# First expert phase of an audio tower: its first weights resident in SBUF, copied per tile by ScalarE, and 101 and 103 tiles in place of 104

## The chip, the core and the metric

The kernel runs on one core of one Trainium2 chip. The metric is the device time of one execution in microseconds (us). TensorE (PE), VectorE (DVE), ScalarE (ACT), GpSimd (POOL) and SyncE (SP) each work through a queue of their own and meet only at semaphores. SP issues plain DMAs, POOL the indirect ones, which scatter rows by an index.

## The reference, cut to what matters

The input is 8 sequences of 750 positions with 128 features. A convolution block leaves 748 positions each, so 5,984 tokens. Two layers of attention-like mixing follow, each with a mixture of experts behind it. The first mixture, which the change is about:

```python
scores = xt @ gate_w.T
_, idx = jax.lax.top_k(scores + biases, K)                       # K = 2 of E = 8 experts
h = jax.nn.silu(jnp.einsum('td,edh->eth', xt, w1)) * jnp.einsum('td,edh->eth', xt, w3)   # 128 -> 256
y = jnp.einsum('eth,ehd->etd', h, w2)                            # 256 -> 128
out = jnp.einsum('te,etd->td', comb, y) + shared
```

The second mixture takes the best 2 of 10 experts with one first weight of 128x512, a bias, an elu and a second weight of 512x128. All data is float32.

## The kernel before

Each token goes to two experts, 11,968 pairs in all. The pairs are sorted by expert in DRAM (`rows_in`), each expert's region padded up to whole tiles of 128 rows, and the program runs through a fixed number of tiles, `EXPERT_TILES` = 104, in both expert phases. A row holds 128 features, the place of its result and its gate. How many tiles an expert has is decided while the program runs; the tables `tile_expert`, `tile_col` (the expert times 128) and `tile_row` are written by VectorE, one entry to a tile, and engines read them into registers. Tiles behind the last real one are empty ones.

A tile `u` of the first phase (`experts0`) passes through these steps. The line numbers are those of the profile:

- SP loads its 128 rows (`load_row`, L708, 65 KB) and its expert's first weights w1 and w3, side by side 128x512, 256 KB (`load_w1`, L713).
- PE transposes the rows (`xT`, L990); DVE copies the result to SBUF (`xT`, L1873).
- PE multiplies by w1 and w3 (`up`, L1001: four products, eight matmul records in float32).
- ACT applies silu to one half (`silu`, L1341), DVE multiplies by the other (`u`, L1879).
- PE multiplies by w2 (`down`, L1010, four records); DVE scales by the gate (`y`, L1900).
- POOL keeps place and gate of the row apart (`keep`, L2224 and L2225) and stores the result rows with an indirect DMA (`store`, L2232).

There are 8 slots (`RING`) for rows, first weights and outputs, and 4 sets of PSUM banks (`SLOTS`), so a slot is used again 8 tiles later. Row loads wait for `keep` of the tile 8 before, weight loads for `u` of the tile 8 before, and `keep` and `y` for the store of the tile 8 before. The second weights of all experts (`ew2_0`) already lie in the tensor `wreg`, loaded at the start; the area from column 2048 to 6144 of `wreg` is unused until the phase is over.

The function `turns` sets the order on each engine: in turn `u` an engine does each of its steps for tile `u + AHEAD[step]`. With `xT` 3, `up` and `silu` 2, `u` 1, `down` and `y` 0, PE's turn is `xT(u+3), up(u+2), down(u)`, DVE's is `xT(u+3), u(u+1), y(u)`, POOL's is `keep(u+3), store(u)`. An engine works in this order alone, so a step that waits holds up everything behind it. Eight turns form one pass of a loop; the last pass stands outside it. The class `Steps` counts each engine's finished steps for each slot on a semaphore.

The second expert phase has the same steps, but its first weights and bias come from DRAM (`w_and_b`, 258 KB a tile), ACT copies xT (L1355) and computes four exponentials (L1348), and PE has 18 matmul records where the first phase has 13.

Of the kernel before, what the change touches and what calls it, by code (L numbers as in the profile page):

```python
# [9 lines left out]
I32 = mybir.dt.int32  # L10
ALU = mybir.AluOpType
# [16 lines left out]
assert (PAIRS + (E1 - 1 + 1) * (P - 1)) // P <= EXPERT_TILES  # L28
# [12 lines left out]
EITERS = EXPERT_TILES // SLOTS  # L41
GROUPS = 2
RING = GROUPS * SLOTS
RITERS = EXPERT_TILES // RING
REGION = (B * L + P - 1) // P + 1
# [38 lines left out]
AHEAD = {"xT": 3, "up": 2, "silu": 2, "exp": 2, "u": 1, "down": 0, "y": 0, "keep": 3, "store": 0}  # L84


def turns(eng, stages, begin=None):
# [25 lines left out]
class Steps:  # L113
# [7 lines left out]
    def __init__(self, phases):  # L121
        self.phases, self.base, self.next = phases, {}, {}
        at = {}
        for phase, (iters, count, names) in phases.items():
            assert len(names) <= self.CREDIT
            for lane in self.lanes(count):
                self.base[phase, lane] = at.get(lane, self.CREDIT)
                at[lane] = self.base[phase, lane] + iters * len(names)
# [18 lines left out]
    def end(self, phase):  # L147
# [4 lines left out]
        return [(lane, self.base[phase, lane] + iters * len(names)) for lane in self.lanes(count)]  # L152


def audio_tower(nc, d, out):
    with ExitStack() as ctx:
# [20 lines left out]
        tile_col = sb("tile_col", [P, EXPERT_TILES], I32)  # L177
# [24 lines left out]
        ew2_0 = wreg[:, 0:E0 * HID0]  # L202
        sw13 = wreg[:, 6144:6144 + 512]
# [298 lines left out]
        def chunk_steps(names):  # L502
# [7 lines left out]
            "experts0": (EITERS, SLOTS, ["xT", "up", "down"]),  # L510
            "attention": (ITERS, LANES, ["norm5T", "q0", "q1", "k0", "k1", "v"]
                          + chunk_steps(["sc", "cx"]) + ["out", "norm6T", "rc1", "taps", "scores"]),
            "experts1": (EITERS, SLOTS, ["xT", "up", "down"]),
# [7 lines left out]
            "experts0": (EITERS, SLOTS, ["silu"]),  # L521
            "attention": (ITERS, LANES, ["n5T", "q0", "q1", "k0", "k1"] + chunk_steps(["qb", "kt", "den"])
                          + ["n6T", "rc1", "taps", "kept"]),
            "experts1": (EITERS, SLOTS, ["xT", "exp"]),
# [7 lines left out]
            "experts0": (EITERS, SLOTS, ["xT", "u", "y"]),  # L532
            "attention": (ITERS, LANES, ["h3", "var5", "norm5", "q0", "q1", "k0", "k1", "v"]
                          + chunk_steps(["at", "st"]) + ["h4", "var6", "norm6", "scores"]),
            "experts1": (EITERS, SLOTS, ["u", "y"]),
# [6 lines left out]
            "experts0": (EITERS, SLOTS, ["keep"]),  # L542
            "attention": (ITERS, LANES, ["rstd5", "rstd6"]),
            "experts1": (EITERS, SLOTS, ["keep"]),
# [103 lines left out]
        def _(sp):  # L648
# [50 lines left out]
            def expert_tiles(m, phase):  # L699
# [1657 lines left out]
```

## Time and profile before

| | |
|---|---|
| median of 3 timed runs | 1641.15 us (1637.29 to 1647.4) |
| profiled execution, its own time | 1635.27 us |
| span of the profiled execution | 1633.4 us |
| TensorE busy in the span | 1331.9 us, 82% |
| VectorE, ScalarE, GpSimd busy | 1011.0, 623.3 and 568.2 us |
| first expert phase, first transpose to last store's start | 393.0 to 583.7 us |
| second expert phase, first to last store's start | 1366.8 to 1572.3 us |

All numbers of the rows are of the one profiled execution. A start is in us from the start of the span. PE is the matmul side of TensorE and PEld its weight loads. Behind a row of a timeline stands in brackets how long the engine had been idle and what released it; "remote" is a release that the profile can't pin to an engine's step. The end of a matmul is modelled.

### The profile page before, as it was taken

How to read it: one execution, taken by the hardware profiler on the slowest of the kernel's cores; microseconds unless marked ns; L12 is line 12 of the kernel's file. 1: busy time of each engine (PE TensorE's matmuls, PEld its weight loads, DVE VectorE, ACT ScalarE, POOL GpSimd, SP SyncE). 2: the span in 40 equal slices, each digit the busy share in tenths (PEclk: the TensorE clock that was granted, in tenths of full speed). 3: DMA queues.
4: the chain of work that ended last, by engine and by line, in shares of the span. 5: the costliest groups of instructions: out<-in, count | busy, mean ns of one | idle time of the engine just before them, and what ended most of it. 6: DMA issues, size and time to landing. Idle time of an engine off the chain costs nothing.

```text
span 1633.4 us, 33209 instructions
## 1 busy us (share of the span) xinstructions
PE 1331.9 (82%) x10360; PEld 1114.8 (68%) x10361; DVE 1011.0 (62%) x3372; ACT 623.3 (38%) x1514; POOL 568.2 (35%) x900
## 2 busy tenths in 40 slices
PE   5687595958888828796899869988699798999975
PEld 3475564736888826575687647876487798999963
DVE  6396777663444457765454745647364546988956
ACT  2425445221222204262234513344235225666633
POOL 1114545535777730002200050001400324777742
PEclk9798797988999969998899989989799899999997
DMA  7102200005777630100010010000101134777734
GB/s 232 49 19 70 54 19 24 28 24 156 218 215 220 212 126 1 40 1 20 20 40 2 1 36 24 20 1 8 32 2 36 38 113 115 193 200 192 199 109 152
DMA packets 104747, 133.18 MB, mean 82 GB/s; under 512 B 21127, under 2 KB 61293, under 8 KB 104386
## 3 DMA queue, kind: packets, MB, share of 16 engines
q1 hardware_dynamic: 91330, 107.08, 22.5%
q0 software_dynamic: 13312, 24.74, 4.5%
q8 instruction: 61, 1.00, 0.3%
q14 instruction: 44, 0.36, 0.1%
HBM read 99.28 MB, written 36.51 MB: 83 GB/s over the span
## 4 chain that ended last, share of the span: by engine, by line
PE 56%; DVE 18%; issue 10%; DVEq 4%; ACT 4%; POOL 3%; DMA 2%; another core or an unknown queue 2%; POOLq 1%; SPq 0%; ACTq 0%
PE psum L1152 10%; PE psum L1001 9%; PE psum L1010 7%; PE psum L1091 3%; PE psum L1068 3%; PE psum L990 3%; DVE work L1556 2%; PE psum L1161 2%; PE psum L1113 2%; DVE stats L1539 2%; PE psum L815 2%; PE psum L1210 2%; PE psum L1086 2%; PE psum L1095 1%
## 5 line engine op out<-in xcount | busy, mean ns | idle before, releaser
L1152 PE MATMUL psum<-NT,wreg 128*128 128x182 f32 (+1 forms) x1536 | 265.3, 329 | 15.9 <-issue 7.9
L1152 PEld LDWEIGHTS psum<-NT,wreg 128*128 128x128 f32 x1536 | 251.6, 194 | 24.4 <-issue 13.5
L1001 PE MATMUL psum<-work 128*128 128x128 f32 x1664 | 225.4, 279 | 24.1 <-DVE work L1873 23.0
L2232 POOL DMA_INDIRECT rows_out<-work,expert_row_kept x208 | 206.2, 991 | 107.5 <-issue 37.5
L2181 POOL TENSOR_TENSOR rstd<-var_eps,pack 128x6 f32<-128x6 f32 x40 | 57.7, 1443 | 496.3 <-DVE var_eps L1546 496.0
L1001 PEld LDWEIGHTS psum<-work 128*128 128x128 f32 x1664 | 204.3, 193 | 31.4 <-issue 17.7
L1348 ACT ACTIVATE work<-psum,work 128x128 f32<-128x128 f32 x416 | 118.6, 368 | 64.4 <-PE psum L1001 56.8
L1900 DVE TENSOR_SCALAR work<-psum,expert_row_kept 128x128 f32<-128x128 f32 x208 | 72.7, 349 | 105.3 <-PE psum L990 47.7
L1891 DVE SCALAR_TENSOR_TENSOR work<-psum,work 128x128 f32<-128x128 f32 x416 | 117.1, 344 | 7.8
L815 PE MATMUL psum<-pack,work 128*128 128x128 f32 (+2 forms) x288 | 54.2, 349 | 80.3 <-DVE work L1556 73.7
L1010 PE MATMUL psum<-work 128*128 x832 | 110.2, 275 | 1.4 <-DVE work L1891 1.4
L2200 POOL DMA_INDIRECT rows_in<-N,slot_now x96 | 99.0, 1031 | 28.6 <-issue 28.4
L815 PEld LDWEIGHTS psum<-pack,work 128*128 128x128 f32 (+2 forms) x288 | 45.3, 185 | 90.2 <-DVE work L1556 56.3
L1010 PEld LDWEIGHTS psum<-work 128*128 128x128 f32 x832 | 101.2, 192 | 2.0 <-issue 2.0
L1341 ACT ACTIVATE work<-psum 128x256 f32<-128x256 f32 x104 | 39.3, 383 | 156.3 <-PE psum L1001 108.5
L2195 POOL TENSOR_TENSOR slots_seen<-pack 128x1 f32<-128x1 f32 x16 | 4.1, 255 | 264.2 <-DVE slot_now L1742 250.5
L1949 DVE TENSOR_TENSOR work<-psum,pack 128x1024 f32<-128x1024 f32 (+1 forms) x48 | 56.7, 1192 | 32.5 <-remote 19.1
L1068 PE MATMUL psum<-work 64*128 64x256 f32 (+1 forms) x384 | 57.8, 422 | 17.1 <-DVE work L1984 9.3
L2224 POOL TENSOR_TENSOR keep_seen<-pack 128x1 f32<-128x1 f32 x208 | 51.1, 246 | 53.5 <-PE psum L990 48.6
L1963 DVE TENSOR_TENSOR upd<-psum,pack 128x128 f32<-128x128 f32 x40 | 11.5, 288 | 86.3 <-PE psum L1095 65.8
L1445 ACT COPY pack<-psum 128x384 f32<-128x384 f32 (+1 forms) x64 | 29.9, 470 | 91.4 <-PE psum L1152 81.1
L1010 PE MATMUL psum<-wreg,work 128*128 x416 | 63.4, 275 | 0.9 <-DVE work L1879 0.9
(358 smaller groups left out, 2837.0 us busy)
## 6 DMA issues: line engine op xcount, KB each, us to landing
work<-w_and_b SPq DMA_DIRECT2D x104, 258.0 KB
work<-in_ew SPq DMA_DIRECT2D x104, 256.0 KB
work<-rows_in SPq DMA_DIRECT2D x208, 65.0 KB
work<-rows_out SPq DMA_DIRECT2D x32, 384.0 KB, 4.3
rows_out<-work,expert_row_kept POOLq DMA_INDIRECT x208
work<-in_xT SPq DMA_DIRECT2D x8, 375.0 KB, 4.7
w_and_b<-in_ew SPq DMA_DIRECT2D x1, 2560.0 KB
out<-H SPq DMA_DIRECT2D x8, 320.0 KB
```

The lines of the kernel that those rows point to most:

```text
L815: r = nc.tensor.transpose((acc or v.P)[:, j // 3, c0:c0 + widths[j]], src(j), ident[0:widths[j], 0:widths[j]])
L1001: r_ = mm(v.ps1[:, c * P:(c + 1) * P], v.w1[:, c * P:(c + 1) * P], v.xT, start=True, stop=True)
L1010: r_ = mm(v.psy, v.e[:, c * P:(c + 1) * P], weights[:, bass.ds(which[u] * nh + c * P, P)], start=(c == 0), stop=(m == 0 and c == nh - 1))
L1068: mm(acc[:, :, 0:n], v.QK[2 + g][rows, col], v.QB[rows, g, :, 0:n], start=True, stop=True)
L1152: r = mm(bank[:, half * HALF_PAIRS:half * HALF_PAIRS + p1 - p0], weights[:, m * P:(m + 1) * P], product_input(name, g, k, p0, p1), start=( ...
L1348: r_ = A(v.e[:, c * P:(c + 1) * P], v.ps1[:, c * P:(c + 1) * P], ACT.Exp, bias=v.b1[:, c:c + 1])
L1891: r_ = V.scalar_tensor_tensor(v.e[:, cols], v.ps1[:, cols], v.b1[:, c:c + 1], v.e[:, cols], ALU.add, ALU.max)
L1900: V.tensor_scalar(v.y, v.psy, v.gate, None, ALU.mult).then_inc(dve_done[k], dve.step(phase, "y", k))
L1949: r = V.tensor_tensor(v.AT2[0:n, :, 0:n], v.AB.rearrange("p b (x i) -> p (b x) i", i=P)[0:n, :, 0:n], w("causal")[0:n, 0:n].unsqueeze(1).b ...
L2181: r = G.tensor_tensor(v.rstd[:], v.ve[:], w("minus_half"), ALU.pow)
L2200: G.indirect_dma_start(rows_in[m], bass.IndirectOffsetOnAxis(ap=slot_now[0:n, q, j:j + 1], axis=0), staged(m, q, k)[0:n, j % TILES, :], No ...
L2232: G.indirect_dma_start(rows_out[m], bass.IndirectOffsetOnAxis(ap=v.dest, axis=0), v.y, None, bounds_check=last, oob_is_err=False).then_inc ...
```

## The change

Three things change.

1. All first weights of the first phase (8 experts, 128x4096, 2 MB) are loaded once, at the start of the program, into the free columns of `wreg` (`ew1_0`). SP's 104 loads L713 are gone, and with them SP's read of `tile_expert` and its wait for DVE's `u` in this phase.
2. ACT gets a step `w1`, three tiles ahead: it copies the tile's 512 columns from `ew1_0` to the slot's `w1`, at an offset that it reads from `tile_col` once in 8 tiles. PE's `up` waits for that copy in place of the load.
3. The number of tiles is worked out for each phase (`EXPERT_COUNT`): (11968 + 8*127)/128 = 101 in the first, (11968 + 10*127)/128 = 103 in the second. The last pass has 5 and 7 turns in place of 8, and semaphore counts are adapted. The tables still have 104 entries, and 4 zeros behind `tile_col`.

```diff
-EITERS = EXPERT_TILES // SLOTS
+EXPERT_COUNT = [(PAIRS + ne * (P - 1)) // P for ne in (E0, E1)]
+LAST_ROUND = [n - (RITERS - 1) * RING for n in EXPERT_COUNT]
-AHEAD = {"xT": 3, "up": 2, "silu": 2, "exp": 2, "u": 1, "down": 0, "y": 0, "keep": 3, "store": 0}
+AHEAD = {"w1": 3, "xT": 3, "up": 2, "silu": 2, "exp": 2, "u": 1, "down": 0, "y": 0, "keep": 3, "store": 0}
...
-            if first and t < 0 or last and t >= RING:
+            if first and t < 0 or last and t >= LAST_ROUND[m]:
...
+        ew1_0 = wreg[:, 2048:2048 + E0 * 2 * HID0]
+        experts0_w1_in = sem("experts0_w1_in")
...
             for name, dst in (("sw13", sw13), ("sw2", sw2)):
                 sp.dma_start(dst, d[name]).then_inc(shared_in, 16)
+            sp.dma_start(ew1_0.rearrange("p (x c) -> p x c", x=E0),
+                         d["ew_0"].rearrange("p (x c) -> p x c", x=E0)[:, :, 0:2 * HID0]).then_inc(experts0_w1_in, 16)
             for t in range(3):
                 sp.dma_start(raw_taps[:, t].rearrange("p (g c) -> p g c", g=3),
...
-                    if m == 0:
-                        sp.dma_start(slots[u].w1, d["ew_0"].rearrange("p (x c) -> p x c", x=E0)[
-                            :, bass.ds(x, 1), 0:2 * HID0].rearrange("p a c -> p (a c)")).then_inc(w1_in[u], 16)
-                    else:
-                        sp.dma_start(slots[u].w1b, w1b_1[bass.ds(x, 1)].rearrange("a p c -> p (a c)")).then_inc(w1_in[u], 16)
+                    sp.dma_start(slots[u].w1b, w1b_1[bass.ds(x, 1)].rearrange("a p c -> p (a c)")).then_inc(w1_in[u], 16)
...
                 def up(u, i):
-                    e.wait_ge(w1_in[u], i * 16 + (16 + m * 16 * RITERS))
                     if m == 0:
+                        e.wait_ge(act_done[k], act.at(phase, "w1", k, r))
                         e.wait_ge(dve_done[k], dve.at(phase, "xT", k, r))
...
+                def begin_w1(at, places):
+                    e.reg_load(regs[0:len(places)], tile_col[0:1, bass.ds(at, len(places))])
+                    for u, place in enumerate(places):
+                        which[place] = e.snap(regs[u], min_val=0, max_val=P * (E0 - 1))
+
+                def w1(u, i):
+                    v = slots[u]
+                    k, r = slot_round(u, i)
+                    e.wait_ge(pe_done[k], pe.at(phase, "up", k, r - GROUPS))
+                    nc.scalar.copy(v.w1, ew1_0[:, bass.ds(which[u] * 4, 4 * P)]).then_inc(act_done[k], act.step(phase, "w1", k))
+
+                e.wait_ge(experts0_w1_in, 16)
+                e.wait_ge(dve_route_done, dve_route.at("tables0", "tables", 0, 0))
+                begin_w1(0, range(ahead))
+                turns(e, [("w1", w1), ("silu", silu)], m, lambda i: begin_w1(i * RING + ahead, [(u + ahead) % RING for u in range(RING)]))
```

On SP, in the first expert phase's loop, row loads and weight loads took turns (L708 is a row load, L713 a weight load, `in_ew` the weights in DRAM, ISA a register step that carries a wait):

```order
L736 TENSOR_LOAD tile_expert
L737 REGISTER_ALU
L737 TENSOR_LOAD tile_row
L740 ISA
L707 ISA
L708 DMA work<-rows_in 128x130
L742 ISA
L711 ISA
L713 DMA work<-in_ew 128x512
```

and now, at the same place, only the row loads are left:

```order
L758 TENSOR_LOAD tile_row
L761 ISA
L729 ISA
L730 DMA work<-rows_in 128x130
L729 ISA
L730 DMA work<-rows_in 128x130
L761 REGISTER_ALU
```

So of every two DMAs that SP issued for a tile one is gone, with one of two table reads in a pass.

On ACT, in the same loop, there was one activation for a tile, the silu:

```order
L98 UNCONDITIONAL_BRANCH
L98 ISA
L1341 ACTIVATE work<-psum 128x256 x2
L1339 ISA
L1341 ACTIVATE work<-psum 128x256 x2
```

and now a copy of another 128x512 stands ahead of each, with a table read at the head of a pass:

```order
L1393 TENSOR_LOAD tile_col
L1395 ISA
L1400 ISA
L1401 COPY work<-wreg 128x512
L1366 ISA
L1368 ACTIVATE work<-psum 128x256
L1400 ISA
L1401 COPY work<-wreg 128x512
```

L1401 is the copy of tile `u+3`'s weights and L1368 the silu of tile `u+2`; between them no function table is loaded.

At the start of the program SP gets one DMA, L683, ahead of the three that bring the convolution taps (L686; before, L664 stood right behind L662):

```order
L679 DMA wreg<-in_ew 128x8x256
L682 DMA wreg<-in_sw 128x512
L682 DMA wreg<-in_sw 128x256
L683 DMA wreg<-in_ew 128x8x512
L686 DMA H<-in_conv 128x3x512 x3
```

So everything that SP issues from L686 on stands behind 2 MB more.

## Rows read from the trace of the kernel before

**Rows 1.** The page, its first line.

```profile
span 1633.4 us, 33209 instructions
```

**Rows 2.** Busy time by stretch: start:end, length, engines, granted clock, DMA share, GB/s.

```profile
420.00:570.00 150.00, 129.30 (x1087) 122.73 (x1088) 71.95 (x252) 31.52 (x84) 109.45 (x250) 1.00 0.72 217
1370.00:1570.00 200.00, 197.52 (x1785) 193.59 (x1785) 180.18 (x600) 132.13 (x493) 144.02 (x297) 1.00 0.68 184
```

**Rows 3.** The line L2232, 388 to 590 us: ns min/median/max, starts, idle before.

```profile
L2232 POOL DMA_INDIRECT rows_out<-work,expert_row_kept x104: 971/992/1029, 400.8 to 583.7; - x104
  DVE work L1873: 34.3, 27
```

**Rows 4.** Waits, 393 to 585 us: us in total, times, longest.

```profile
ACT work L1341 <- PE psum L1001: 108.5, 73, 12.6
DVE work L1900 <- remote: 36.8, 17, 2.4
PE psum L1001 <- DVE work L1873: 23.0, 29, 1.1
```

**Rows 5.** Timeline, 469.8 to 474.9 us: start, busy us, engine, line, idle before.

```profile
470.07 1.06 PE L1001 MATMUL psum<-work 128*128 128x128 f32 x8
...
470.56 0.99 POOL L2232 DMA_INDIRECT rows_out<-work,expert_row_kept  x1 [0.16 <-issue]
...
470.96 0.61 PE L1010 MATMUL psum<-wreg,work 128*128 x4
...
471.52 1.06 PE L1001 MATMUL psum<-work 128*128 128x128 f32 x8
471.58 0.20 POOL L2224 TENSOR_TENSOR keep_seen<-pack 128x1 f32<-128x1 f32 x1
...
471.94 0.38 ACT L1341 ACTIVATE work<-psum 128x256 f32<-128x256 f32 x1 [1.84 <-PE psum L1001]
472.06 1.00 POOL L2232 DMA_INDIRECT rows_out<-work,expert_row_kept  x1 [0.16 <-issue]
...
473.43 0.35 DVE L1900 TENSOR_SCALAR work<-psum,expert_row_kept 128x128 f32<-128x128 f32 x1 [2.20 <-remote]
...
474.57 0.99 POOL L2232 DMA_INDIRECT rows_out<-work,expert_row_kept  x1 [1.18 <-DVE work L1873]
```

**Rows 6.** The line L2232 in the second expert phase, 1300 to 1620 us.

```profile
L2232 POOL DMA_INDIRECT rows_out<-work,expert_row_kept x104: 966/991/1030, 1366.8 to 1572.3; - x104
```

**Rows 7.** Waits, 1366 to 1573 us.

```profile
ACT work L1348 <- PE psum L1001: 56.8, 90, 0.8
```

**Rows 8.** DMA, 393 to 585 us: SP's queue (packets, MB, share), its issues of weights.

```profile
q1 hardware_dynamic: 28276, 31.96, 57.5%
...
work<-in_ew SPq DMA_DIRECT2D x96, 256.0 KB
```

**Rows 9.** Groups by line and form on ACT, whole span: busy us, mean ns.

```profile
L1341 ACT ACTIVATE work<-psum 128x256 f32<-128x256 f32 x104 | 39.3, 383 | 156.3 <-PE psum L1001 108.5 <-remote 29.4 <-issue 18.3
L1355 ACT COPY work<-psum 128x128 f32<-128x128 f32 x104 | 27.6, 266 | 8.1 <-PE psum L990 5.0 <-issue 3.1
...
L1414 ACT COPY work<-work 128x640 f32<-128x640 f32 x8 | 5.8, 726 | 0.0
```

**Rows 10.** The line L981 on PE's sequencer, 388 to 590 us.

```profile
L981 PEldq TENSOR_LOAD <-tile_col x13: 588/617/775, 394.5 to 567.7; - x13
```

**Rows 11.** Timeline, the start of the first expert phase.

```profile
391.65 1.02 DVE L1838 TENSOR_TENSOR H<-psum,H 128x640 f32<-128x640 f32 x2 [0.24 <-PE psum L957]
...
394.05 2.05 PE L1001 MATMUL psum<-work 128*128 128x128 f32 x8 [0.35 <-DVE work L1873]
```

**Rows 12.** Timeline, the start of the program.

```profile
8.21 3.11 SPq L664 DMA_DIRECT2D H<-in_conv  x3
...
29.98 1.75 DVE L1845 TENSOR_TENSOR N<-H 128x1536 f32<-128x1536 f32 x1
```

**Rows 13.** DMA issues, 0 to 35 us: KB each, median us from issue to landing.

```profile
H<-in_conv SPq DMA_DIRECT2D x3, 768.0 KB, 10.3
```

**Rows 14.** Busy time by stretch, the start of the program.

```profile
13.00:23.00 10.00, 9.27 (x25) 2.91 (x25) 3.18 (x20) 6.21 (x7) 0.00 (x0) 1.00 0.85 301
```

More of the change, by code:

```diff
@@ L44 @@
 RITERS = EXPERT_TILES // RING
+LAST_ROUND = [n - (RITERS - 1) * RING for n in EXPERT_COUNT]
+assert all(4 <= n <= RING for n in LAST_ROUND)
 REGION = (B * L + P - 1) // P + 1
@@ L80, with rounds, rounds_upto, slot_rounds @@
     _place(_n, _r, _c)
-AHEAD = {"xT": 3, "up": 2, "silu": 2, "exp": 2, "u": 1, "down": 0, "y": 0, "keep": 3, "store": 0}
-def turns(eng, stages, begin=None):
+AHEAD = {"w1": 3, "xT": 3, "up": 2, "silu": 2, "exp": 2, "u": 1, "down": 0, "y": 0, "keep": 3, "store": 0}
+def rounds(m, u):
+    return RITERS - 1 + (u < LAST_ROUND[m])
+def rounds_upto(m, u):
+    return sum(rounds(x, u) for x in range(m))
+def slot_rounds(m):
+    return [rounds(m, k) + rounds(m, k + SLOTS) for k in range(SLOTS)]
+def turns(eng, stages, m, begin=None):
     def run(i, u, first=False, last=False):
@@ L127, in __init__, with count_of @@
                 self.base[phase, lane] = at.get(lane, self.CREDIT)
-                at[lane] = self.base[phase, lane] + iters * len(names)
+                at[lane] = self.base[phase, lane] + self.count_of(iters, lane) * len(names)
+    @staticmethod
+    def count_of(iters, lane):
+        return iters[lane] if isinstance(iters, list) else iters
     @staticmethod
@@ L734, in expert_tiles, with reload @@
                     load_row(u)
-                with sp.Fori(1, RITERS) as i:
-                    sp.reg_load(regs, tile_expert[0:1, bass.ds(i * RING, RING)])
+                def reload(i, count):
+                    if m == 1:
+                        sp.reg_load(regs, tile_expert[0:1, bass.ds(i * RING, RING)])
                     sp.reg_load(rows, tile_row[0:1, bass.ds(i * RING, RING)])
-                    for u in range(RING):
+                    for u in range(count):
                         k, r = slot_round(u, i)
@@ L741, in expert_tiles @@
                         load_row(u)
-                        sp.wait_ge(dve_done[k], dve.at(phase, "u", k, r - GROUPS))
-                        load_w1(u)
+                        if m == 1:
+                            sp.wait_ge(dve_done[k], dve.at(phase, "u", k, r - GROUPS))
+                            load_w1(u)
+                with sp.Fori(1, RITERS - 1) as i:
+                    reload(i, RING)
+                reload(RITERS - 1, LAST_ROUND[m])
             def w2_of(x0, x1):
@@ L1014, in down @@
                     r_.then_inc(pe_done[k], pe.step(phase, "down", k))
-                turns(e, [("xT", xT), ("up", up), ("down", down)], begin)
+                turns(e, [("xT", xT), ("up", up), ("down", down)], m, begin)
             barrier(e, "mix_a")
@@ L1355, in xT @@
                     nc.scalar.copy(v.xT, v.psx).then_inc(act_done[k], act.step(phase, "xT", k))
-                turns(e, [("silu", silu)] if m == 0 else [("xT", xT), ("exp", exp)])
+                if m == 1:
+                    turns(e, [("xT", xT), ("exp", exp)], m)
+                    return
+                ahead = AHEAD["w1"]
+                regs = [e.alloc_register(f"{phase}_w1_expert{u}") for u in range(RING)]
+                which = {}
+                def begin_w1(at, places):
[11 more added lines that the diff above has]
+                turns(e, [("w1", w1), ("silu", silu)], m, lambda i: begin_w1(i * RING + ahead, [(u + ahead) % RING for u in range(RING)]))
             expert_tiles(0, "experts0")
@@ L1512, in _ @@
             V.memset(not_first[:], 1.0)
+            V.memset(tile_col[:, EXPERT_TILES:], 0)
             V.memset(tiny[:], 1e-6)
@@ L2233, in store @@
                                          bounds_check=last, oob_is_err=False).then_inc(row_stored[u], 16)
-                turns(e, [("keep", keep), ("store", store)])
+                turns(e, [("keep", keep), ("store", store)], m)
             store_rows(0, "experts0")
```

52 lines of the change are left out of this document (27 added, 25 removed).

## The prediction

> **What bounds the kernel now.** I read the page first, and then the busy time by stretch, to see where the change lies. The span is 1633.4 us [rows 1]. The first expert phase is one ninth of it, and in its steady part no engine is full: of 150 us PE is busy 129.30, DVE 71.95, ACT 31.52 and POOL 109.45, at full granted clock [rows 2]. In the second phase PE is busy 197.52 of 200 us [rows 2]: that one is bound by PE, the first by something else.
>
> The line of the stores tells the pace of the first phase, because each tile ends with one. 104 stores start between 400.8 and 583.7 us [rows 3]: 182.9 us for 103 steps, 1.776 us a tile. The timeline shows that this is a mean over two kinds of step. Stores start at 470.56 and 472.06, which is 1.50 us, and the next at 474.57, which is 2.51 us [rows 5]. The 1.50 us is POOL's own floor: 0.99 us of store, then `keep`, then 0.16 us before the next store. PE's floor lies just beneath it: its `up` starts at 470.07 and at 471.52, so 1.45 us a turn [rows 5]. The long step is a wait of POOL for DVE's `y`, and POOL waits so 27 times, 34.3 us in all [rows 3]. At 1.50 us throughout, 103 steps would take 154.5 us, so 28.4 us of the phase are such stalls.
>
> What makes `y` late is not work. `down` is modelled to end at 470.96 + 0.61 = 471.57, yet `y`, with DVE idle for 2.20 us, starts at 473.43, 1.86 us later, and its release is one that the profile calls "remote" [rows 5]. ACT's silu shows the same: `up` ends at 470.07 + 1.06 = 471.13, the silu that waits for it starts at 471.94, 0.81 us later [rows 5]. In the phase `y` waits 17 times for a "remote" release, 36.8 us; PE then waits 29 times for DVE's `xT`, 23.0 us, since that stands behind the late `y` in DVE's queue [rows 4]. So releases arrive late, while POOL stores without a pause and the DMA queues are full. DMAs come three to a tile: rows, weights, store.
>
> The second phase has the same three DMAs a tile, and the same store of 991 ns, over 205.5 us for 103 steps, 1.995 us a tile [rows 6]. There ACT's longest wait for `up` is 0.8 us [rows 7], against 12.6 us in the first (that longest one is the wait at its start), and no "remote" waits stand among the long ones. So the delay is there at 3 DMAs in 1.776 us (1.69 a us) and not at 3 in 1.995 us (1.50 a us).
>
> **The change, part by part.**
>
> *The loads that go.* Of the 31.96 MB on SP's queue in the phase, 96 loads of 256 KB are weights, 25.2 MB [rows 8]. What is left is two DMAs a tile. Even at POOL's floor, 2 in 1.50 us, that is 1.33 a us, less than the second phase's 1.50, which runs without these delays. The trace of before can't show the mechanism, so the gain is bounded from both sides: nothing (the stores alone cause the delays; 1.776 us a tile stays) and all of it (1.50 us a tile). I take the end near 1.50, since the second phase, the nearest case in rates, is free of the stall: 100 steps at 1.50 us, 150.0 us, and 5 us for what follows next. In place of 182.9 us that is 155.0, so **-27.9 us**; of this 3 steps at 1.776, 5.3 us, are the fewer tiles.
>
> The Trainium skill speaks against this part. Its page "SBUF — State Buffer", section "Who interferes with whom", says that a DMA never contends with a compute engine. By that, taking away loads which nobody waits for would give nothing, and the phase would only lose its three tiles. The trace does not name a matmul that waits for a weight load, which agrees, but it shows releases 0.81 and 1.86 us late [rows 5], which the rule has no place for.
>
> *The copy on ACT.* The trace has no 128x512 copy from SBUF to SBUF. A copy of 640 columns takes 726 ns and one of 128 takes 266 [rows 9]: 0.90 ns a column, so about 0.61 us for 512 (an estimate from these two; 0.27 and 0.73 are its bounds). With the silu of 383 ns [rows 9] ACT has 1.0 us of work a tile, and 1.5 us of time. ACT's turn is `w1(u+3)`, `silu(u+2)`: the copy runs while ACT would otherwise wait for `up(u+2)`, and `up(u+3)` comes a full turn of PE later. So it is hidden, cost 0. Its wait, for `up` of the tile 8 before, is over long before. If that cover is gone, PE waits for ACT; see the slower rival.
>
> *The table read.* Once in 8 tiles ACT reads registers; PE does the same with 617 ns [rows 10]. With the copy and the silu behind it that is 0.62 + 0.61 + 0.38 = 1.6 us in that turn, 0.1 more than the turn has. It delays a silu, which has most of a turn to spare until `down` needs it, but PE has only 0.05 us a turn to catch up with. Between nothing and 12 x 0.62 = 7.4 us; the 5 us above are for this and for a few remaining late releases.
>
> *Start of the phase.* ACT can begin only when the phase before is over, as PE can: DVE's last add ends about 392.7 us (391.65 us, two adds), and the first `up` starts at 394.05 [rows 11]. ACT has to read its registers and copy once, 0.62 + 0.61 = 1.2 us [rows 9, 10], and some waits ahead of it: **+0.5 us**, bounds 0 and 1.9.
>
> *The 2 MB at the start.* They stand ahead of the taps. At the 301 GB/s of that stretch [rows 14] they take 7.0 us. The taps are all issued by 11.3 us and land 10.3 us later [rows 12, 13], about 21.6; now about 28.6. DVE uses them first at 29.98 [rows 12]. Cost 0, with 1.4 us of cover left; DVE would wait if the stretch ran slower, some 2 us at most.
>
> *SP, POOL and DVE.* SP loses half its issues in the loop, and rows are no longer issued behind a wait for `u`. POOL and DVE have the same steps, three tiles fewer. The `memset` of four columns costs nothing.
>
> *The second phase* has 103 tiles: one step of 1.995 us less [rows 6], **-2.0 us**. It stays bound by PE [rows 2].
>
> The sum is -27.9 + 0.5 - 2.0 = -29.4 us. The profiled execution took 1635.27 us, which lies 5.9 us under the median of the timed runs, and would come to 1605.9. Carried over to the median, 1641.15 - 29.4 gives **1611.7 us**, 1.8% faster.
>
> **The rivals.**
>
> *Stalls thin out, but stay.* Late releases might depend on POOL's back-to-back stores as much as on the loads. With a third fewer DMAs I would then keep, as an estimate between the bounds, about half of the 28.4 us: 14 us more than the forecast's 150, less its 5, so 1611.7 + 9 = 1621, up to 1626. For it: the stores are unchanged and leave no gap at 1.50 us a tile. Against it: the rate argument above.
>
> *No relief.* The loads have nothing to do with the delay, and 1.776 us a tile stay: -5.3 + 0.5 - 2.0 = -6.8 us, **1634 us**, within 1%. This is also what the skill's rule on DMA and compute gives. For it: no row says that a weight load is waited for. Against it: the second phase has the same stores, and not the waits.
>
> *Slower: ACT closes a loop.* `w1(u+4)` stands on ACT behind `silu(u+2)`, which waits for `up(u+2)`; and `up(u+4)` waits for that copy. This loop of two tiles takes `up` 1.06, the late release, the silu 0.38, the copy 0.61 and some 0.05. With a release 0.81 us late it is 2.9 us, under 3.0 for two tiles, and harmless; with 1.86 us on each [rows 5] it is 3.96, so 1.98 us a tile, 100 steps in 198 us: 15.1 more than before, less 2.0, plus 0.5, **1655 us**. It decides from a mean delay of about 1.45 us on (two tiles at 1.776). Before, only some releases were that late, and the waits of ACT average 108.5/73 = 1.5 us mostly because it has nothing else to do [rows 4].
>
> **How the numbers follow.** The forecast has a chance of 0.58, its own range 1605 (all steps at 1.50, no cost elsewhere: 1641.15 - 32.9 - 2.0 = 1606, and a little for the scatter of runs) to 1618. Stalls thin out: 0.22. No relief: 0.14. The loop on ACT: 0.06. The range of 1602 to 1630 leaves out the last two and holds the first two. About 1% is what a measurement of this kernel can tell from no change; that is 1624.7. Faster by more than 1%: 0.58 and most of the 0.22, 0.77. Within 1%: 0.18. Slower: 0.05.
>
> **What would show it.** In the profile of the changed kernel the stores should start 1.50 us apart nearly throughout, so that POOL's line L2232 (by its new number) spans 150 to 160 us in place of 182.9; POOL's waits for DVE should fall from 34.3 us to under 10, and `y`'s "remote" waits from 36.8 to a few. The copy should take 0.6 us and PE should hardly wait for it. DVE's first use of the taps should stay near 30 us. The prediction is wrong if the stores keep steps of 2.5 us every few tiles though SP issues rows alone, or if PE's `up` is released by ACT's copy with idle time ahead of it.

## The result, and the profile after

The changed kernel took 1649.49 us (median of 20 runs, 1631.91 to 1654.65), the kernel before 1636.66 us (20 runs, 1628.41 to 1647.4): ratio 1.0072, 95% interval 1.0052 to 1.0091. It is slower by 0.7%, where 1.8% faster was forecast. On two other chips, where the kernel before takes 1655 to 1657 us, the ratio was 1.001 (0.9987 to 1.0033) and 1.0008 (0.9988 to 1.0028): no difference. On no chip is there a gain.

The changed kernel's page, first line; the profiled execution took 1643.51 us:

```profile
span 1641.7 us, 33304 instructions
```

Busy time by stretch (columns as in [rows 2], which these two answer):

```profile
420.00:570.00 150.00, 129.00 (x1093) 123.05 (x1094) 73.69 (x252) 75.22 (x169) 109.92 (x252) 1.00 0.27 72
1370.00:1570.00 200.00, 196.95 (x1772) 192.23 (x1772) 178.83 (x591) 131.09 (x491) 146.26 (x292) 1.00 0.68 188
```

The change did what it says: the DMA share of the first phase fell from 0.72 to 0.27, 217 to 72 GB/s, and ACT's work more than doubled (31.52 to 75.22 us), by one copy a tile. But PE and POOL are busy for the same 129 and 110 us as before: the pace is nearly the same. The line of the stores, in the first and in the second phase (compare [rows 3] and [rows 6]):

```profile
L2282 POOL DMA_INDIRECT rows_out<-work,expert_row_kept x101: 975/991/1029, 408.2 to 584.6; - x101
  DVE work L1923: 31.3, 22
...
L2282 POOL DMA_INDIRECT rows_out<-work,expert_row_kept x103: 975/989/1029, 1372.0 to 1578.5; - x103
```

In the first phase 176.4 us for 100 steps, 1.764 us a tile (before: 1.776; forecast: 1.50). In the second 206.5 us for 102 steps, 2.025 us a tile (before: 205.5 for 103, 1.995). The waits, 393 to 585 us, total, times, longest (compare [rows 4]):

```profile
DVE work L1950 <- remote: 35.9, 17, 2.5
...
ACT work L1401 <- issue: 25.7, 12, 2.2
...
PE psum L1028 <- ACT work L1401: 7.0, 6, 1.7
```

DVE's `y` waits for "remote" releases as before: 17 times, 35.9 us, against 17 times, 36.8 us. The profile uses that name where a release comes over 1.5 us after the modelled end of every step that could have given it; a smaller delay is put down to a PE step. So "remote" counts only the longest delays. Two waits are new. ScalarE stands 2.2 us "for issue" 12 times, once a round of 8 tiles, and PE waits for the copy. The timeline shows one of each (start, busy us, idle before in brackets):

```profile
470.59 0.35 DVE L1950 TENSOR_SCALAR work<-psum,expert_row_kept 128x128 f32<-128x128 f32 x1 [2.40 <-remote]
470.72 0.61 ACT L1401 COPY work<-wreg 128x512 f32 x1
...
471.46 1.15 PE L1028 MATMUL psum<-work 128*128 128x128 f32 x8 [1.18 <-ACT work L1401]
...
476.72 0.62 ACT L1401 COPY work<-wreg 128x512 f32 x1 [2.23 <-issue]
477.39 1.16 PE L1028 MATMUL psum<-work 128*128 128x128 f32 x8 [1.32 <-issue]
```

Most of those 2.2 us is the table read, which stands on its sequencer (duration in ns, least, median, most). PE reads 8 columns in 617 ns [rows 10]; ScalarE takes three times as long:

```profile
L1393 ACTq TENSOR_LOAD <-tile_col x14: 905/1802/1899, 398.6 to 574.8; - x14
```

### The profile page after: what moved, and what is told of

The parts are those of the page before. It is cut to its first block, busy times and chain, and to the rows that moved or that the text cites. A ratio compares the mean times of both kernels' runs of the same rounds, so it can differ in the third digit from the quotient of the medians.

```text
span 1641.7 us, 33304 instructions
## 1 busy us (share of the span) xinstructions
PE 1329.9 (81%) x10303; PEld 1109.0 (68%) x10304; DVE 1010.4 (62%) x3358; ACT 673.1 (41%) x1608; POOL 565.6 (34%) x888
## 4 chain that ended last, share of the span: by engine, by line
PE 48%; issue 23%; DVE 14%; POOL 4%; DVEq 3%; ACT 2%; DMA 2%; another core or an unknown queue 1%; POOLq 1%; SPq 0%; ACTq 0%
PE psum L1028 11%; PE psum L1037 8%; PE psum L1179 6%; POOL rows_in L2250 3%; PE psum L1066 2%; DVE work L1606 2%; PE psum L1016 2%; PE psum L1237 2%; PE psum L841 2%; PE psum L1118 2%; PE psum L1095 1%; DVE stats L1589 1%; PE psum L1188 1%; PE psum L972 1%
## 5 line engine op out<-in xcount | busy, mean ns | idle before, releaser
L1179 PEld LDWEIGHTS psum<-NT,wreg 128*128 128x128 f32 x1536 | 251.5, 194 | 29.5 <-issue 20.8
L2282 POOL DMA_INDIRECT rows_out<-work,expert_row_kept x204 | 202.2, 991 | 103.6 <-issue 41.7
L1028 PEld LDWEIGHTS psum<-work 128*128 128x128 f32 x1632 | 201.2, 194 | 34.6 <-issue 16.2
L2250 POOL DMA_INDIRECT rows_in<-N,slot_now x96 | 97.9, 1019 | 28.6 <-issue 28.4
L1037 PEld LDWEIGHTS psum<-work 128*128 128x128 f32 x824 | 100.3, 192 | 2.0 <-issue 2.0
L1401 ACT COPY work<-wreg 128x512 f32 x101 | 61.7, 612 | 38.1 <-issue 25.7
L1368 ACT ACTIVATE work<-psum 128x256 f32<-128x256 f32 x101 | 38.7, 383 | 63.1 <-PE psum L1028 38.6
L2013 DVE TENSOR_TENSOR upd<-psum,pack 128x128 f32<-128x128 f32 x40 | 11.6, 289 | 85.6 <-PE psum L1122 63.0
```

Source lines behind the costliest of these rows:

```text
L1028: r_ = mm(v.ps1[:, c * P:(c + 1) * P], v.w1[:, c * P:(c + 1) * P], v.xT, start=True, stop=True)
L1037: r_ = mm(v.psy, v.e[:, c * P:(c + 1) * P], weights[:, bass.ds(which[u] * nh + c * P, P)], start=(c == 0), stop=(m == 0 and c == nh - 1))
L1179: r = mm(bank[:, half * HALF_PAIRS:half * HALF_PAIRS + p1 - p0], weights[:, m * P:(m + 1) * P], product_input(name, g, k, p0, p1), start=( ...
L1401: nc.scalar.copy(v.w1, ew1_0[:, bass.ds(which[u] * 4, 4 * P)]).then_inc(act_done[k], act.step(phase, "w1", k))
L2250: G.indirect_dma_start(rows_in[m], bass.IndirectOffsetOnAxis(ap=slot_now[0:n, q, j:j + 1], axis=0), staged(m, q, k)[0:n, j % TILES, :], No ...
L2282: G.indirect_dma_start(rows_out[m], bass.IndirectOffsetOnAxis(ap=v.dest, axis=0), v.y, None, bounds_check=last, oob_is_err=False).then_inc ...
```

## The experiments

All ratios are to the kernel before on the same chip, with 95% intervals. A step is the first phase's, from the first and last start of the stores. A round is 8 tiles, from start to start of DVE's `y`. The name in brackets behind "Measured", as (e1), is short for the run. Steps and waits come from one trace a run.

**1. The parts of the change, one at a time.** The counts alone: `EXPERT_COUNT` and the partial last rounds, with the weights loaded for each tile as before.

> The 101 and 103 tiles alone; the first weights are loaded for each tile as before, no load at the start, no copy on ScalarE. The traces give both kernels about the same step in the first phase (1.776 and 1.765 us a store), so three tiles fewer there are worth 3 x 1.77 = 5.3 us and one fewer in the second 2.0 us. Theory A (the counts gain what they should, the residency costs the rest): 1636.7 - 7.3 = 1629.4 us, ratio 0.9955. Theory B (what the changed kernel lost is in the partial last rounds and the instructions that now lie twice, in and behind the loop): 1640 us or more, ratio 1.002 to 1.008, and in the trace the second phase's step is 2.02 us as in the changed kernel instead of 1.995.

Measured (e1): 0.9957 (0.9933 to 0.9981), step 1.844 us; second phase 205.7 us for 102 steps, no shorter than before's 205.5. Theory A's ratio holds, but the gain is in the first phase alone: in the second a round of 8 takes 16.25 us in place of 16.09, 12 times 0.16 us, and that eats the tile. PE is busy for 197 of 200 us there, so a few more instructions of its sequencer at the round's end might show at once, but no run shows it. Against it stands that the run (s2) below has the changed kernel's instructions on PE in this phase, and rounds of 16.18 us where the changed kernel has 16.33. The cause is open.

The residency alone, 104 tiles in both phases:

```
-EXPERT_COUNT = [(PAIRS + ne * (P - 1)) // P for ne in (E0, E1)]
+EXPERT_COUNT = [EXPERT_TILES, EXPERT_TILES]
```

> The changed kernel with 104 tiles in both phases, so the residency alone: 2 MB at the start, the copy on ScalarE, no load for a tile in the first phase. Theory A: what it costs shows without the gain of the counts, 1649.5 + 7.3 = 1656.8 us, ratio 1.012. Theory B (the last rounds cost): 1649.5 us or less, ratio under 1.008. In both the first phase's step stays at 1.76 to 1.78 us, 27 to 30 of the steps over 1.6 us, since the late releases do not come from the loads.

Measured (e2): 1.0006 (0.9987 to 1.0025), step 1.860 us, 38 of the 103 over 1.6 us. A's 1.012 is missed. B's bound is kept, but not for its reason, since the last rounds alone cost nothing above.

The kernel before with the 2 MB load at the start added:

```
             for name, dst in (("sw13", sw13), ("sw2", sw2)):
                 sp.dma_start(dst, d[name]).then_inc(shared_in, 16)
+            sp.dma_start(ew1_0..., d["ew_0"]...[:, :, 0:2 * HID0]).then_inc(experts0_w1_in, 16)
```

> The kernel before with one addition: the 2 MB load at the start at the place of the changed kernel, into columns that nobody reads in that time; the weights are still loaded for each tile. Theory A1 (the load at the start delays the mixing stage, by some 5.4 us at 306 us and 6 us at the first row load as the pair of traces shows): 1636.7 + 6 = 1642.7 us, ratio 1.0037, and the first row load at 395.8 us instead of 389.8. Theory A2 (the load is free and the lag before the first phase comes from something else, such as how the instructions are fetched): 1636.7 us, ratio 1.000, first row load at 390 us.

Measured (e3): 1.0003 (0.9983 to 1.0024), and yet the first row load is at 396.0 us. The changed kernel with that load late:

> The changed kernel with the 2 MB load moved to behind the x loads of the mixing stage on SP's queue, ahead of the loads for the second phase's weights; everything else as changed. Theory A1: the lag of 5 to 6 us before the first phase is gone, 1649.5 - 6 = 1643.5 us, ratio 1.004. Theory A2: 1649.5 us, ratio 1.007, and the first row load still at about 396 us.

Measured (e4): 1.0005 (0.9981 to 1.0029), first row load still at 396.3 us. So the load is not what makes it late. The stretch from 60 to 160 us shows what does. The first row is the kernel before (first trace), the second the kernel before from another execution, b_before below; granted clock is the third column from the end:

```profile
60.00:160.00 100.00, 78.24 (x436) 56.94 (x437) 62.47 (x254) 50.42 (x89) 26.96 (x27) 0.86 0.09 27
```

```profile
60.00:160.00 100.00, 78.59 (x401) 52.78 (x402) 59.09 (x249) 51.06 (x91) 24.46 (x25) 0.82 0.06 18
```

The same kernel runs the mixing stage with a mean granted clock of 0.86 or of 0.82, and does 436 or 401 matmuls in that stretch. The first row load follows: 389.8 us at 0.86, 395.2 at 0.82. Over the twenty traces of this case it lies between 387.6 and 393.8 us in the eight at 0.86, and between 395.2 and 397.7 in the twelve at 0.82; kernels with the load at the start are in both groups (387.6 and 390.6, 395.8 and 396.0). The 6 us by which the changed kernel's first phase began later in the first pair of traces are such a difference between executions, not the load's.

**2. The changed kernel again, and a trace of the kernel before from the same chip.**

> The changed kernel once more, beside the kernel before on the same chip, so that the variants can be compared with it. Alone the counts gave ratio 0.9957, alone the residency 1.0006. Theory C (the parts add up, the rest of the first result is TensorE's clock pattern, which differs from execution to execution): the ratio is between 0.996 and 1.007, and over the executions the time falls by 10 to 15 us where the mean granted clock is 0.01 higher. Theory D (counts and residency together cost something of their own): ratio 1.007 again, also between executions of the same clock.

Measured (a_after_again): 1.001 (0.9987 to 1.0033). The parts would make 0.9957 times 1.0006, 0.9963, so they don't quite add up; why not is open. The step was 1.940 us, with the mean granted clock at 0.93 between 450 and 550 us. That trace is of one of the longest executions, 1666.71 us for a median of 1657.24. PE's waits for the copy came to 20.8 us (the 41 and 11 us of an expectation below add those of the weight loads, which run beside them).

> The kernel before, unchanged, for a trace from the same chip as the changed kernel's. If the chip matters for the late releases (the kernel before with a load added had a step of 1.840 us on another chip where the first trace has 1.776), the step is 1.80 to 1.85 us here; if not, 1.77 to 1.79 us.

> The changed kernel a third time. If the parts cancel (counts -0.4%, ScalarE's read and copy and the later start +0.4 to +1.1%), the ratio is between 1.000 and 1.007; the step of the first phase is 0.00 to 0.10 us longer than in the kernel before on the same chip, and the waits of PE for ScalarE's copy make 10 to 45 us.

Measured: 1657.08 us (b_before, one execution), and 1.0008 (0.9988 to 1.0028) for the changed kernel (a_after_third). The stores' line in b_before and in a_after_third:

```profile
L2232 POOL DMA_INDIRECT rows_out<-work,expert_row_kept x104: 969/992/1030, 408.1 to 598.6; - x104
```

```profile
L2282 POOL DMA_INDIRECT rows_out<-work,expert_row_kept x101: 975/991/1029, 401.9 to 589.7; - x101
```

190.5 us against 187.8: the step is 1.850 and 1.878 us, on a chip where `y` of the kernel before waits 26 times for a "remote" release instead of 17. Three tiles fewer, 5.5 us, give 2.7. The rest goes to a longer step, and the second phase and the end give 1.2 and 1.7 us away.

Over the 20 executions of the changed kernel on the first chip, time and mean granted clock go together: from 1631.91 us at 0.913 to 1654.65 at 0.904. A straight line through all 20 gives 14 us for 0.01, correlation -0.86. On the chip of a_after_again it is 13.5 us. So C's range and its slope hold, its adding up of the parts does not, and D's 1.007 did not return. What the clock does not explain is the median on the first chip: there the changed kernel's median clock was 0.905, the profiled execution of the kernel before had 0.913. Why that chip favours the kernel before stays open.

**3. What makes the releases late.** The changed kernel with the first phase's stores as plain DMAs from SP. Rows go to the wrong places, and POOL only copies gate and row numbers:

```
-turns(e, [("keep", keep), ("store", store)], m)
+turns(e, [("keep", keep)] if m == 0 else [("keep", keep), ("store", store)], m)
...
+sp.wait_ge(dve_done[k], dve.at(phase, "y", k, r))
+sp.dma_start(rows_out[0][bass.ds(at * P, P)], slots[u].y).then_inc(plain_stored[u], 16)
```

> The changed kernel with the first phase's stores put on SP as plain DMAs of a tile to a fixed place (so the rows go to the wrong places and the output is not the reference's); POOL only copies gate and row numbers there. Theory S: no row of DVE L19xx waits for a release that comes over 0.6 us late, the first phase's step is 1.50 to 1.56 us, set by PE. Theory P: step 1.74 to 1.80 us with POOL nearly idle.

Measured (s2): 1633.08 us, one execution. Its waits between 410 and 540 us, the largest, and the line of `y`:

```profile
ACT work L1382 <- PE psum L1042: 36.9, 68, 0.6
...
ACT work L1415 <- issue: 22.9, 10, 2.3
...
PE psum L1042 <- ACT work L1415: 11.8, 10, 1.2
```

```profile
L1964 DVE TENSOR_SCALAR work<-psum,expert_row_kept x101: 345/351/352, 400.8 to 565.5; 128x128 f32<-128x128 f32 x101
```

No wait is put down to a "remote" release any more, and between 410 and 540 us the longest wait of the silu is 0.6 us. In the trace's semaphore events all of PE's 279 releases from 410 us to the end of the phase now come within 0.05 us of the modelled end. With POOL's stores 89 of 254 did in the changed kernel, 43 of 250 before (410 to 560 us; some events are missing from those traces, so the rest is only a rough count). The step is 1.647 us, not 1.50. The rounds from the third to the eleventh take 13.22 to 13.25 us; within a round a turn of ScalarE is 1.449 us, which would be 11.6. The missing 1.66 us are at one place:

```profile
467.66 0.62 ACT L1415 COPY work<-wreg 128x512 f32 x1 [2.30 <-issue]
...
468.33 0.94 PE L1042 MATMUL psum<-work 128*128 128x128 f32 x6 [1.20 <-ACT work L1415]
```

The same edit in the kernel before, so with its 25 MB of weight loads:

> The kernel before with the first phase's stores put on SP as plain DMAs of a tile to a fixed place (the rows go to the wrong places, so the output is not the reference's), weights loaded for each tile, 27 MB of loads as before. Theory S (POOL's stores cause the late releases, the loads do not): no wait for a release that comes late, a round of 8 tiles in 12.4 us every time, step 1.55 us, since the same edit in the changed kernel gave 13.25 us with 0.9 us of it at the place where ScalarE reads the table. Theory L (the loads make them late too): rounds of 13 us and more that differ from each other, late releases at over 10 places.

Measured (s1): 1662.4 us, one execution, step 1.898 us. No late release either (all 231 of PE's between 410 and 560 us come within 0.05 us), so the loads don't cause them. But a new bound came in: rows and stores share SP's queue with 256 KB of weights a tile, and PE waits for rows.

```profile
PEld psum L1002 <- DMA work<-rows_in: 37.5, 52, 1.8
PE psum L1002 <- DMA work<-rows_in: 26.7, 38, 1.6
```

Both theories thus missed the pace; on the cause of the late releases S holds, with two limits. The edit takes away POOL's store instruction and the scattered write together, and which of the two matters was not tested. And the stores are not enough by themselves. In the second phase of the kernel before the same stores run, 1.995 us apart, and of PE's 223 releases between 1400 and 1550 us the trace has 188 events, all within 0.05 us. In the first phase only PE's releases are late: all 175 events of DVE's and all 42 of ACT's between 420 and 570 us come within 0.05 us. What the first phase adds is open.

**4. The table read.** ScalarE reads one column behind each SiLU, instead of 8 at the end of a round:

```
-e.reg_load(regs[0:len(places)], tile_col[0:1, bass.ds(at, len(places))])
...
+def read(u, i):
+    e.reg_load(regs[u:u + 1], tile_col[0:1, bass.ds(i * RING + u, 1)])
...
+turns(e, [("w1", w1), ("silu", silu), ("read", read)], m)
```

First with the plain stores (rows to the wrong places again):

> The changed kernel with plain stores on SP (rows go to the wrong places) and the read spread. Theory R: rounds of 8 tiles fall from 13.25 to 11.6 to 11.9 us, step 1.45 to 1.50 us. If the round stays at 13.2 us, something else at the round's end (PE's own read of 0.6 us, the jump back) costs the 1.66 us.

Measured (m3): 1611.64 us, one execution on a chip where the kernel before takes 1656.59 (that it comes next to the forecast's 1611.7 is chance). Busy time by stretch, and the line of `y`:

```profile
420.00:540.00 120.00, 120.00 (x1063) 119.15 (x1062) 72.62 (x246) 81.69 (x163) 25.76 (x164) 1.00 0.35 90
```

```profile
L1960 DVE TENSOR_SCALAR work<-psum,expert_row_kept x101: 346/351/353, 402.5 to 548.0; 128x128 f32<-128x128 f32 x101
```

145.5 us for 100 steps, 1.455 us a tile, rounds of 11.77 us, PE busy all the time. Theory R holds: the read cost 1.5 us a round, 19 us in the phase. This is the phase that the forecast had in mind, and it is there only when both POOL's stores and the long read are gone. Then with POOL's stores, so the kernel's full work:

> The changed kernel with one edit: ScalarE reads the table column of one tile at a time, behind each SiLU, instead of 8 columns in one read (1.75 us) at the end of each round. Theory R (that read is what eats the residency's and the counts' gain): up to 12 x 1.7 = 20 us off, so a step of 1.65 to 1.75 us and ratio 0.988 to 0.994. Theory S alone (late releases hold the step whatever ScalarE does): step 1.76 to 1.85 us as with the counts alone, ratio 0.996 to 1.000.

Measured (m1): 0.9989 (0.9970 to 1.0008), step 1.837 us. A single read takes 0.28 us:

```profile
L1391 ACTq TENSOR_LOAD <-tile_col x101: 273/279/487, 400.0 to 584.9; - x101
```

Theory S alone, on this one. Beside late releases spreading the read brings nothing that can be told from noise (the changed kernel had 1.001 and 1.0008 on its chips): the read falls into stalls that are there anyway.

**5. The copy.** The changed kernel without copy and read (PE takes the weights of a fixed expert, so products are with the wrong ones):

> The changed kernel without the copy and the read: PE takes the up weights from a fixed place of the resident table, place u of the ring those of expert u, so tiles are multiplied by the wrong expert's weights; all else as changed. It is what the residency could give at best with POOL's stores. Theory S alone: the late releases stay, step 1.74 to 1.84 us, ratio 0.994 to 0.997, as the counts alone. Forecast's theory (the loads caused the late releases and ScalarE's part brought them back): step 1.50 us, ratio 0.982.

```profile
L2261 POOL DMA_INDIRECT rows_out<-work,expert_row_kept x101: 978/994/1030, 408.5 to 584.2; - x101
```

Measured (m4): 0.9921 (0.9891 to 0.9950), step 1.757 us on the chip where the spread read has 1.837. The late releases stay: set against the modelled end of its own `down`, `y` starts over 0.3 us late, with DVE idle, 34 times of 101, against 37 of 104 in the kernel before. The best that resident weights and the counts together could give with these stores is 0.8%. Copy and short read cost 0.08 us a tile, 8 us, though the copy was forecast to be hidden. Is it PE's wait for the copy? A copy 5 tiles ahead, not 3, takes that wait away:

```
-AHEAD = {"w1": 3, "xT": 3, ...
+AHEAD = {"w1": 5, "xT": 3, ...
```

> The changed kernel with one number changed (and the list of table columns lengthened for it): ScalarE copies a tile's weights 5 tiles ahead instead of 3. With 3, the up product of a tile waits for a copy that stands only one turn before it, behind a SiLU whose release may be late and, once in 8 tiles, behind the read of the table; PE's waits for that copy were 41 us in the changed kernel's second trace and 11 us in its first, in no kernel with loaded weights. Theory Q (this closed loop between PE and ScalarE eats what the counts give): PE's waits for the copy under 5 us, no stretch of low clock within the phase, the step down to that of the kernel with the counts alone (1.78 to 1.85 us against 1.77 to 1.94), ratio 0.993 to 0.997. Theory C (clock pattern and chance): step and ratio as in the changed kernel, 1.000 to 1.003.

Measured (l1): 0.999 (0.997 to 1.0009), step 1.806 us. PE's waits for the copy fell to 1.2 us. Three of Q's signs came, the short waits, the clock and the step, but not its ratio: the time can't be told from the kernel before's, nor from the changed kernel's. So this wait is at most a small part of what the copy costs. What is left is that ScalarE has 1.0 us of work a tile to catch up with after a late release, instead of 0.38; this is argued, not shown.

The clock went with that wait. In five of the six traces with POOL's stores, the long read and the copy 3 tiles ahead the mean granted clock between 420 and 550 us is 0.947 to 0.987; in the sixth, the first trace of the changed kernel, and in the other fourteen it is 1.00. In a_after_again the clock fell from 2.4 to 1.2 GHz three times in the phase, each time in or just behind a wait of PE of 3.0 to 3.2 us for the copy. What this is worth in time was not separated.

**6. Gaps for POOL.** The copy of gate and row numbers goes from POOL to DVE in the first phase, so that POOL has time between stores:

```
+V.tensor_copy(v.dest, v.row[:, P:P + 1].bitcast(I32))
+V.tensor_copy(v.gate, v.row[:, P + 1:ROW]).then_inc(dve_done[k], dve.step(phase, "keep", k))
...
+turns(e, [("store", store)] if m == 0 else [("keep", keep), ("store", store)])
```

> The kernel before with one edit in the first expert phase: the copy of a tile's gate and row numbers goes from POOL to DVE, so POOL only stores; a store's row then has about 0.99 us of DMA_INDIRECT and 0.5 us or more in which POOL does nothing. Theory S (other engines' releases get through late while POOL's stores follow each other without a gap): the late releases vanish and the step falls from 1.776 to about 1.55 us, the 1.53 to 1.55 us that PE is busy for a tile; 103 x 0.22 = 23 us off, ratio 0.986. Theory P (PE's own chain with DVE and ACT sets 1.76 us, POOL only follows): step 1.74 to 1.80 us, ratio 0.998 to 1.003.

Measured (k1): 0.9953 (0.9930 to 0.9976), step 1.780 us. It helps, by a third of what S named. The late releases did not vanish: `y` starts over 0.3 us late 44 times of 104.

> The changed kernel with the same edit: the copy of gate and row numbers goes from POOL to DVE in the first expert phase. Theory S: step 1.765 to about 1.55 us, 100 x 0.21 = 21 us off the changed kernel, ratio 0.987 to 0.994 to the kernel before by where the changed kernel stands beside it. If here the step is lower than in the variant made from the kernel before, the loads that the change removed matter once POOL has gaps. Theory P: step as in the changed kernel.

Measured (k2): 1.008 (1.0051 to 1.0109), step 1.928 us: in the changed kernel, which has 1.001 on this chip, the same edit hurts.

> The changed kernel with the copy 5 tiles ahead and the copy of gate and row numbers on DVE. With weights loaded, the latter gave ratio 0.9953; in the changed kernel it made 1.008 out of 1.001. Theory Q (the loop through ScalarE's copy is what made it worse): with the lead of 5 it helps here too, ratio 0.990 to 0.994, step 1.70 to 1.78 us. Otherwise (DVE's additional work in the way of the releases that PE waits for): ratio 1.003 or more.

Measured (l3): 0.999 (0.9972 to 1.0009), step 1.856 us; the lead takes the harm away, and brings no gain.

> The changed kernel with the read spread over the tiles and the copy of gate and row numbers on DVE. Theory R and S together (both causes gone): rounds of 8 tiles in about 12 us, step 1.47 to 1.60 us, 20 to 30 us off the changed kernel, ratio 0.980 to 0.988. Otherwise, if gaps in POOL's work don't free the releases in a kernel with resident weights, ratio 0.995 or more.

Measured (m2): 0.9961 (0.9939 to 0.9982), step 1.809 us, so R and S together fall. `y` and the silu still have late releases:

```profile
ACT work L1368 <- remote: 26.9, 12, 2.4
DVE work L1957 <- remote: 22.6, 11, 2.3
```

And with loaded weights and the counts:

> The kernel before with two edits and no residency: 101 and 103 tiles, and gate and row numbers copied by DVE in the first phase. Each alone gave ratios 0.9957 and 0.9953. If they add up: ratio 0.991, 1641 us where the kernel before takes 1655; the step of the first phase 1.75 to 1.78 us. If the counts' gain in the first phase was the tiles alone and the second phase gives nothing (its rounds of 8 tiles are 16.24 us with the counts and 16.09 us without), the sum is 0.992.

Measured (k3): 0.9945 (0.9923 to 0.9968), 1647.53 us where the kernel before takes 1656.91. The ratio is the lowest with the full work, but can't be told from those of the two edits alone (0.9957 and 0.9953), and the sum of both, 0.991 or 0.992, did not come. Step 1.709 us; the waits for "remote" releases are almost gone:

```profile
DVE work L1935 <- PE psum L1013: 59.8, 47, 1.7
...
ACT work L1364 <- remote: 6.4, 2, 3.3
DVE work L1935 <- remote: 5.3, 3, 2.0
```

The first of these lines says that this is not the end of the late releases. Before, it read:

```profile
DVE work L1900 <- PE psum L990: 37.9, 31, 2.2
```

`y` waits for `down`; the profile names the transpose (L1013, L990) because that had ended last when the release came. Measured against the end of its own `down`, `y` starts over 0.3 us late 47 times of 101 in k3 and 37 of 104 in the kernel before, but over 1.5 us late 3 times and 19 times. In the semaphore events between 410 and 560 us, 48 of 263 of PE's releases come within 0.05 us, as few as the 43 of 250 before. So a gap of 0.3 us between the stores cut the longest delays here and did not free the releases; in k1 and m2 even of the longest 12 and 11 are left at `y`. What sets the length of a delay is open, and so is why it is PE's releases that come late. Lead, spread read and DVE's copy together in the changed kernel were not tried.

## Why the prediction was wrong

- **The loads that go (-27.9 us): this step failed.** The observation was right (releases 0.8 to 1.9 us late at 28.4 us of cost), its cause was not. I had two things that differ from the second phase, DMAs a us and POOL's pauses, and chose the DMAs by a rate of 1.69 against 1.50 a us. That "the DMA queues are full" was no reason either: [rows 2] has a DMA share of 0.72 in the first phase and 0.68 in the second. A third difference stands in the same rows and was not weighed, PE busy for 129.30 of 150 us against 197.52 of 200. The run with loads and without POOL's stores has no late release (s1); the ones with a third of the traffic and POOL's stores have them as before. In place of 1.50 us a tile the first phase took 1.764, 6.5 us less than before and not 27.9. The "No relief" rival had this mechanism right, with 1.776 us a tile kept, at a chance of 0.14. Its -6.8 us came with the counts alone (0.9957, 7.1 us), not with the whole change.
- **The Trainium skill's rule.** The Trainium skill, page "SBUF — State Buffer", section "Who interferes with whom", says that DMAs don't contend with compute engines. The trace agrees: with 145 GB/s taken away, PE is busy for 129.00 us where it was 129.30. I set it aside for 1.86 us of lateness, which stayed when the traffic went.
- **The table read (within 5 us): mis-sized.** I took PE's 617 ns for ScalarE's; it takes 1802 ns. Where nothing else stalls, it costs 1.5 us a round, 19 us. With late releases it hides.
- **The copy (0): duration right, cover wrong.** 610 ns against an estimate of 0.61 us. But leaving copy and short read out was worth 0.7% on one chip (0.9989 to 0.9921). The cover I named, ScalarE's wait for `up`, is of no use after a late release; that this is the reason is argued, not shown.
- **The slower rival (1655 us at 0.06).** Its place was right, PE waits for a copy behind a late silu (7.0 us here, 20.8 and 22.4 us in the later traces), and 1649.5 and 1657 us were measured. That its 1655 lies between them is luck: on the chips of 1657 the kernel before takes as long. Its mechanism was not shown: without that wait the time can't be told from the same (l1).
- **Start of the phase (+0.5):** from the first row load to the first store it takes 12.4 us in place of 11.0, +1.4, inside the bounds.
- **The 2 MB at the start (0): right.** DVE's first use of the taps came at 30.34 us in place of 29.98, and the load alone gave 1.0003.
- **The second phase (-2.0): wrong by 3 us.** A tile fewer, and each round 0.24 us longer: +1.0 us. I had called it bound by PE and took a round to stay as long as it was; why it grew is open.
- **Within the first pair of traces** the ends are 8.3 us apart: +6.0 from the mixing stage's clock (between executions), +1.4 at the start of the phase, -6.5 in it, +4.3 from its end to the second phase, +1.0 in that and +2.1 behind it. The medians on this chip are 12.8 apart, and what makes the rest of that has no trace. The causes of the 4.3 and the 2.1 were not found; in the third pair of traces (b_before, a_after_third) they are -1.7 and +1.7.

## What to carry to other kernels

When releases are late and two things distinguish the slow stretch from a quick one, take each away by itself before a redesign is built on one of them: here the two runs with plain stores told. Look also at a stretch that has the suspect and is quick, here the second phase, before the suspect is called the whole cause. A register read on another engine has another price, so take it from that engine, and spread it where an engine's turn is tight. A new instruction on an engine that is idle on average may not be hidden if that engine must catch up after each stall (argued above, not shown). And a name in a wait list can have a threshold: count the delays themselves before a wait is called gone.

## What the runs showed of the hardware

- While POOL issues indirect stores (0.99 us each) in the first phase, PE's semaphore releases reach DVE's `y` up to 1.92 us late in the kernel before and 2.05 in the changed one; with plain stores from SP in their place, all within 0.05 us, with 80 or with 201 GB/s beside them. In the second phase, with the same indirect stores, all 188 recorded ones come within 0.05 us too.
- Reading 8 table columns into registers takes ScalarE 1.76 to 1.96 us (medians of the traces), PE 0.59 to 0.68 and SP 0.52; one column takes ScalarE 0.28.
- The mixing stage runs at a mean granted clock of 0.86 or of 0.82 from one execution to the next of the same kernel; the first row load behind it comes 5.8 us later at 0.82, in the mean of twelve traces against eight.
- The kernel before takes 1637 us on one chip and 1655 to 1657 on five others, where its first phase has a step of 1.850 us (one trace) instead of 1.776.
